# Weight parts with a buffer of their own, a last down projection in two portions, re-placed projections, and group 0's maxima by tiles

## The reference, cut to what matters

```python
x = x + _layernorm(_L0_attn_ref(_layernorm(x), ...))   # stage A: small 4-layer convolution net
x = x + _layernorm(_L0_ffn_ref(_layernorm(x), ...))    # stage B: silu(x W1) * (x W3), then W2, plus rank-2 parts
x = x + _layernorm(_L1_attn_ref(_layernorm(x), ...))   # stage C: causal attention, 32 heads of 32, 8 KV heads
x = x + _layernorm(_L1_ffn_ref(_layernorm(x), ...))    # stage D: x W_org plus 8 blended rank-64 updates

q = jnp.dot(x, Wq).reshape(b, t, H, HD).transpose(0, 2, 1, 3)
scores = jnp.where(causal, -jnp.inf, jnp.einsum('bhqd,bhkd->bhqk', q, k))
weights = softmax(scores * (1.0 / HD ** 0.5))
```

## Time and profile before

| | us |
|---|---|
| median of 3 runs | 2153.36 (2153.06 to 2156.35) |
| the profiled execution | 2154.8 |
| its span, first to last instruction | 2153.0 |
| PE busy | 2002.1 (93%) |
| DVE busy | 1423.2 (66%) |
| POOL busy | 1064.7 (49%) |
| ACT busy | 933.4 (43%) |
| mean granted clock of PE | 0.973 |

### The profile page before, as it was taken

How to read it: one execution, slowest core, us unless ns; L and a number is a source line. 1 busy time by engine, 2 the same in 40 slices (tenths; PEclk the granted TensorE clock), 3 DMA queues, 4 the chain that set the end, 5 groups by cost and what they waited for, 6 DMA issues and landing times. The chain is left out here.

```text
span 2153.0 us, 30681 instructions
## 1 busy us (share of the span) xinstructions
PE 2002.1 (93%) x10444; PEld 1451.0 (67%) x10444; DVE 1423.2 (66%) x3201; ACT 933.4 (43%) x1938; POOL 1064.7 (49%) x914
## 2 busy tenths in 40 slices
PE   5889886999999999989999899999998999999998
PEld 4644545778788878855666466665654687888887
DVE  7877667777777763177776477677776677654433
ACT  5645685333333323115554455555555433323211
POOL 1444586666666530008886488688884343220000
PEclk9999988999999999989999999999998999999999
DMA  6400376244444338532334643433253385543432
GB/s 188 173 9 1 121 232 230 94 151 167 162 167 167 123 129 305 156 95 57 79 81 111 188 117 80 113 98 97 64 165 117 95 271 183 180 168 132 142 123 97
DMA packets 153435, 292.12 MB, mean 136 GB/s; under 512 B 28750, under 2 KB 69582, under 8 KB 153152
## 3 DMA queue, kind: packets, MB, share of 16 engines
q1 hardware_dynamic: 124224, 241.93, 35.4%
q10 hardware_dynamic: 29056, 48.24, 6.8%
HBM read 163.48 MB, written 94.90 MB: 120 GB/s over the span
## 5 line engine op out<-in xcount | busy, mean ns | idle before, releaser
L2253 ACT ACTIVATE c_P<-PS 128x512 f32<-128x512 f32 (+3 forms) x768 | 349.1, 496 | 342.0 <-PE PS L2086 193.2
L2068 PE MATMUL PS<-c_K,c_Q 96*128 96x512 f32 (+3 forms) x768 | 276.8, 371 | 20.2 <-DVE cst L2385 8.8
L2086 PE MATMUL PS<-c_Q,c_K 97*128 97x512 f32 (+3 forms) x768 | 275.7, 373 | 17.1 <-ACT c_P L2253 9.8
L2498 POOL TENSOR_TENSOR c_S<-c_S,c_P 128x1024 f32<-128x1024 f32 (+3 forms) x94 | 242.0, 2575 | 20.3 <-DVE c_S L2334 12.9
L2086 PEld LDWEIGHTS PS<-c_Q,c_K 97*128 97x128 f32 x768 | 147.4, 193 | 140.0 <-ACT c_P L2253 96.3
L2381 DVE TENSOR_REDUCE cst<-PS 128x1 f32<-128x512 f32 x256 | 175.8, 687 | 77.0 <-PE PS L2068 76.7
L2068 PEld LDWEIGHTS PS<-c_K,c_Q 96*128 96x128 f32 x768 | 149.9, 195 | 77.0 <-DVE cst L2385 28.8
L214 POOL TENSOR_TENSOR maskw<-maskw,mhalf 128x1 f32<-128x1 f32 x64 | 37.7, 590 | 329.9 <-DVE maskw L172 317.6
L1432 DVE SCALAR_TENSOR_TENSOR b_pr<-b_g,b_a 128x460 f32<-128x460 f32 x192 | 180.8, 977 | 1.7
L2385 DVE CUSTOM_DVE_ANT_0 PS<-PS,maskw,cst 128x128 f32<-128x128 f32 (+3 forms) x256 | 142.8, 558 | 53.2 <-PE PS L2068 34.0
L2475 POOL TENSOR_SCALAR_AFFINE_SELECT c_P<-c_P 128x512 f32<-128x512 f32 x128 | 87.4, 683 | 159.8 <-ACT c_P L2253 159.8
(11 more groups left out here) (305 smaller groups left out, 4845.5 us busy)
## 6 DMA issues: line engine op xcount, KB each, us to landing
pre_d<-b_pre ACTq DMA_DIRECT2D x36, 512.0 KB, 2.8
c_w<-pre_d SPq DMA_DIRECT2D x34, 512.0 KB, 4.0
a_xin<-in_x SPq DMA_DIRECT2D x32, 512.0 KB, 4.3
d_x<-scr SPq DMA_DIRECT2D x32, 512.0 KB, 4.8
c_Q<-c_qh SPq DMA_DIRECT2D x240, 64.0 KB, 2.0
scr<-a_xin SPq DMA_DIRECT2D x16, 512.0 KB, 5.7
b_xn<-scr SPq DMA_DIRECT2D x16, 512.0 KB, 6.7
b_x<-scr SPq DMA_DIRECT2D x16, 512.0 KB, 5.8
```

The source lines that it names most:

```text
L2068: e.matmul(bank[:, 0:hi - lo], self.Q4[0:96, 4 * (o % 3) + g, 128 * t:128 * t + 128], self.K4[0:96, HEADS[o % 8], lo:hi], start=True, stop ...
L2086: e.matmul(self.k.bank(i % 3)[:, 0:hi - lo], self.K4[0:97, HEADS[o % 8], 128 * kt:128 * kt + 128], self.Q4[0:97, 4 * (o % 3) + g, lo:hi], ...
L2253: e.activation(self.P[:, R % 3, g, 0:hi - lo], self.k.bank(i % 3)[:, 0:hi - lo], ACT.Exp, scale=SCALE).then_inc(self.exp_s.s, 1)
L2498: e.tensor_tensor(S[:, gs, 512 - n:512], S[:, gs, 512 - n:512], P[:, gs, 0:n], ADD).then_inc(self.psum_s.s, 1)
```

## The change

1. Stage B: `raw` has a buffer of its own; a load waits only for the subtraction of the part before, the cast waits for the store. In ACT's list silu comes first, then the other work of the chunk, then cast, load and store of the parts; POOL's subtraction stands one chunk later. The two reductions of `dve_acc` share one `prod`, so the second waits for the first.
2. The end of stage B: `pe_gtr(15, 0)` stands ahead of the last chunk; the down projection runs in two portions, chunks 0 to 3 of both halves, then `pe_gtr(15, 1)`, then chunks 4 and 5.
3. Stage C's begin: group 0's maxima go by tiles (four heads of tile 0, then of tile 1, ...) from step 4 of projection 3 on, evenly over 27 steps (before: head by head, from step 10, over 22). The first 16 need only the first half of Q and K. SP places both halves of projection 0 ahead of the weight loads.
4. Slots: projections' second halves begin 2 slots later; K2, query 7, the reloads and most loads of the output weights move; `dve_job` stands one slot later; `late` and one `pool_mul` are set for group 5 too; stage D's tiles and splits move by 1 to 3 slots.

```diff
-            with nc.sbuf_tensor("b_raw", [128, 2, 512], F32) as raw:
-                self.raw = raw[:, 1, :]
+            self.raw = sb("raw", [128, 512])[:, :]
-            self.prod = [sb("pr0", [128, 460])]
-            self.prod.append(sb("pr1", [128, 460]))
+            self.prod = sb("pr1", [128, 460])
...
-    def pe_down(self, e, t, s):
+    def pe_down(self, e, t, s, pieces=range(6)):
         if s == 0:
-            e.wait_ge(*self.glo_s(2 * t + 2))
+            e.wait_ge(*self.glo_s(2 * t + (2 if 5 in pieces else 1)))
...
-        for i in range(2):
-            self.pe_gtr(e, 15, i)
+                if (t, c) == (15, 4):
+                    self.pe_gtr(e, 15, 0)
         for s in range(2):
-            self.pe_down(e, 15, s)
+            self.pe_down(e, 15, s, range(4))
+        self.pe_gtr(e, 15, 1)
+        for s in range(2):
+            self.pe_down(e, 15, s, (4, 5))
...
-        s = 6 * t + c - 9 - step
+        s = 6 * t + c - 10 - step
     def act_pre_load(self, e, p):
         if p > 0:
-            e.wait_ge(*self.pre_out(p))
+            e.wait_ge(*self.pre_lo(p))
     def act_pre_hi(self, e, p):
         e.wait_ge(*self.pre_in(p + 1))
+        if p > 0:
+            e.wait_ge(*self.pre_out(p))
...
-            if p > 0:
-                e.wait_ge(*self.u2_s(2 * p - 1 + r))
+            if p > 0 or r > 0:
+                e.wait_ge(*self.u2_s(2 * p + r))
...
-    return o, q_slots(48 * o - 112, 2, 48 * o - 94, 2), (48 * o - 95, 48 * o - 73)
+    return o, q_slots(48 * o - 112, 2, 48 * o - 92, 2), (48 * o - 95, 48 * o - 72)
-         ("K2", q_slots(208, 1, 219, 1), (217, 228)), (7, q_slots(231, 1, 243, 1), (242, 260)), ...
+         ("K2", q_slots(208, 1, 220, 1), (218, 233)), (7, q_slots(235, 1, 247, 1), (245, 262)), ...
-WO_IN = {644 + 6 * c: c for c in range(8)}
-TILES = {711 + 4 * n: (0, n) for n in range(8)} | {745 + 4 * n: (1, n) for n in range(5)}
+WO_IN = {643: 0} | {656 + 6 * c: c for c in range(1, 8)}
+TILES = {714 + 4 * n: (0, n) for n in range(8)} | {747 + 4 * n: (1, n) for n in range(5)}
-        late = 5 if S >= 720 or 432 <= S < 480 else 0
+        late = 5 if S >= 720 or 240 <= S < 288 or 432 <= S < 480 else 0
...
+    def max_of(self, o, a):
+        return (a % 4, MAXES[a // 4]) if o == 0 else (a // 12, MAXES[a % 12])
...
-            for o, a in ahead[max(0, 60 * (q - 10) // 22):max(0, 60 * (q - 9) // 22)]:
+            for o, a in ahead[max(0, 60 * (q - 4) // 27):max(0, 60 * (q - 3) // 27)]:
...
-                if S in self.evac_at:
-                    self.dve_job(e, *self.evac_at[S])
+                if S - 1 in self.evac_at:
+                    self.dve_job(e, *self.evac_at[S - 1])
-                if S == 704:
+                if S == 707:
                     for half in range(2):
                         self.then.dve_lo(e, 0, half)
...
-                if o > 0 and r in ((0, 7) if o in (9, 15) else (0, 4)):
+                if o > 0 and r in ((0, 7) if o in (5, 9, 15) else (0, 4)):
                     self.pool_mul(e, 2 * o - (2 if r == 0 else 1))
```

More of the change, by code:

```diff
@@ L1180, in pe_down @@
         o = self.k.bank(6 + s)
-        for c in range(6):
+        for c in pieces:
             a, b = self.gfh[0:115, c, :], self.gfl[0:115, c, :]
@@ L1340, in act @@
             for c in range(6):
-                last, now, p = (self.pre_at(t, c, step) for step in (2, 0, 1))
-                if last is not None:
-                    self.act_pre_store(e, last)
+                now, p, last = (self.pre_at(t, c, step) for step in range(3))
+                if (t, c) == (15, 5):
+                    self.act_ghi(e, 15, 0)
                 self.act_silu(e, t, c)
-                if p is not None:
-                    self.act_pre_hi(e, p)
                 if c in (0, 2):
@@ L1361, in act @@
                     T.act_x(e, t - 2)
+                if p is not None:
+                    self.act_pre_hi(e, p)
                 if now is not None:
                     self.act_pre_load(e, now)
+                if last is not None:
+                    self.act_pre_store(e, last)
                 if t == 1 and c == 5:
@@ L1369, in act @@
                     T.act_y(e, t - 1, y)
-        for i in range(2):
-            self.act_ghi(e, 15, i)
+        self.act_ghi(e, 15, 1)
         T.act_x(e, 14)
@@ L1429, in dve_acc @@
             a = 2 * C0[c] + n * r
-            if p > 0:
-                e.wait_ge(*self.u2_s(2 * p - 1 + r))
-            e.scalar_tensor_tensor(out=self.prod[r][:, 0:n], in0=g, scalar=0.5, in1=self.a2[:, a:a + n], op0=MUL, op1=MUL,
+            if p > 0 or r > 0:
+                e.wait_ge(*self.u2_s(2 * p + r))
+            e.scalar_tensor_tensor(out=self.prod[:, 0:n], in0=g, scalar=0.5, in1=self.a2[:, a:a + n], op0=MUL, op1=MUL,
                                    accum_out=self.u2[:, r, c:c + 1]).then_inc(self.u2_s.s, 1)
@@ L1491, in dve @@
                     self.dve_u2(e, t)
-        for i in range(2):
-            self.dve_glo(e, 15, i)
+        self.dve_glo(e, 15, 1)
         T.add(e, 14)
@@ L2058, in pe_turn, with max_of @@
         return self.turn_bank(o, a)
+    @staticmethod
+    def max_of(o, a):
+        return (a % 4, MAXES[a // 4]) if o == 0 else (a // 12, MAXES[a % 12])
     def pe_amax(self, e, o, a):
-        g, (t, lo, hi) = a // 12, MAXES[a % 12]
+        g, (t, lo, hi) = self.max_of(o, a)
         for part in range(2):
-            if a == 0:
+            if a == (16 * part if o == 0 else 0):
                 e.wait_ge(*self.placed[part](12 * o + 12))
-            if a == 0 and o in (0, 8, 12):
-                e.wait_ge(*self.k4[part]({0: 24, 8: 36, 12: 48}[o]))
+                if o in (0, 8, 12):
+                    e.wait_ge(*self.k4[part]({0: 24, 8: 36, 12: 48}[o]))
         bank = self.pe_turn(e, o, a)
@@ L2306, in act @@
                     self.then.act_hi(e, 0, (S - 699) // 2)
-                if S in (727, 743):
-                    self.then.act_hi(e, 1, int(S > 727))
+                if S in (728, 744):
+                    self.then.act_hi(e, 1, int(S > 728))
                 if S == 758:
                     self.then.act_y(e, 0)
-                if S == 760:
+                if S == 762:
                     self.then.act_hi(e, 2, 0)
```

27 lines of the change are left out of this document (15 added, 12 removed).

## The result

| | before | changed |
|---|---|---|
| median, us | 2154.64 (4 runs, 2153.06 to 2156.35) | 2129.70 (4 runs, 2128.92 to 2130.70) |
| span of the profiled execution | 2153.0 | 2127.7 |
| PE busy | 2002.1 | 1987.9 |
| DVE busy | 1423.2 | 1406.6 |

The ratio is 0.9884, 95% interval 0.9867 to 0.9901: 24.9 us less. Measured once more beside later experiments it was 0.9888 (0.9871 to 0.9904). The forecast was 2126.0, the range 2114 to 2140.

The account below looks back on a forecast made before the run. PE was taken as the bound, able to save only idle time and the half clock behind it. The terms summed to -27.7 us, 2127.1 from 2154.8 or 2125.7 from the median; the forecast was 2126.0, range 2114 to 2140.

Parts of the forecast that it names:

- Stage B: Stage B's weight parts: PE's waits for ACT's copy of the transposed input mostly go; -3.0 us, between -3.6 and +3.
- End of B: End of stage B: the split down projection delays DVE's list and PE idles 6.8 us; +5 us, between -1 and +7.
- Start of C: Start of stage C: maxima begin earlier, first score at about 948, SP ending last; -9.5 us, between -11 and -5.
- Group 5: Group 5, stage C: row of maxima issued ahead of K2, -7.7 us; POOL's sums ahead of its multiplication, -5.5 us.
- small waits for +2.5: New small waits from closer reloads and second halves two slots later: +2.5 us, a guess, between 0 and 5.
- Small waits in C: Stage C: splits on DVE stand behind the maxima a slot later, so PE waits less; -2 us, between -4 and +2.
- Group 14: Group 14, stage C: twelve slots without weight loads free its late row of maxima; -2 us, between -4.4 and 0.
- End of C: End of stage C: stage D's two splits go behind group 15's last maxima; -5.5 us, between -7.5 and -3.2.
- (a): Rival: start of C realised only by a third, projection 3's weights or SP's queue late; 2132.5 us, chance 0.12.
- (b): Rival: the end of stage B costs nothing, -1 instead of +5; 2120 us, chance 0.07.
- (d): Slower rival, stage B: ACT's casts wait for load and store, delaying PE's copy; +34 us, 2163, chance 0.05.
- (c): Rival: half of 22.7 us of removed stalls in stage C given back through POOL or DVE; 2138 us, chance 0.08.

Follow-up runs that it names:

- the second one with the list of before: The kernel before with only the first part of the change, stage B's buffers and order of ACT and POOL, against the kernel before: ratio 0.9978.
- the second trace of the same kernel: The changed kernel itself once more, unaltered, run beside the kernel with four edits: 2134.40 us, ratio to before 0.9888.

## Why the prediction was right, and where it was not

That the total came so near is in part luck: group 5 fell 7.5 us short of its terms, and smaller gains above forecast in stage B, at its end, at the start of C and at the end of C made up for 5.7 of that in this pair of traces. The largest of them, 2.9 us at the end together with group 14, is gone in four of the six other traces of the same list.

- **The bound.** PE's busy list is the same and the gain is waits and clock. Right.
- **Stage B.** Forecast -3.0; -3.9 in the first trace, and 421.0 as the mean of eleven traces with this part against the 424.2 of before, -3.2. The slower rival (casts waiting for load and store) was free of effect: ACT does wait for a store 12 times, 19.6 us, but behind the work that PE needs:

```profile
ACT b_g L1315 <- PE PS L1154: 58.5, 31, 4.9
...
ACT b_pre L1281 <- DMA pre_d<-b_pre: 19.6, 12, 2.0
```

  The step that failed is the price on DVE, which was in the bound only. I had up to 19 us more for the dependent reductions; they took less than before, 158.8 us busy and 5.0 idle against 179.3 and 1.7 for 190 of them:

```profile
L1437 DVE SCALAR_TENSOR_TENSOR b_pr<-b_g,b_a 128x460 f32<-128x460 f32 x190 | 158.8, 836 | 5.0
```

  From the start of the first to the end of the second, a pair has a median of 1.58 us in both kernels, so the wait between them costs nothing that shows. What fell is the time beside POOL. Before, 36 of the 95 pairs ran beside POOL's subtraction of a weight part and took 2.14 us on average, the others 1.74; with that subtraction a chunk later 12 pairs did and took 1.80, the others 1.70. The prediction had no term for that.
- **End of B.** Forecast +5, between -1 and +7; measured +3.9. The chain went as written: 6.71 us idle where I had 6.8. PE was about 3.5 us late at tile 2's transposes (forecast 4.1), and the half clock behind it cost 0.4 more than before (forecast 0.9). It did not cost more because PE's next wait, 1.64 us at tile 3, took most of it; the prediction had PE back to back there and nothing to absorb it. The row at 813.84 agrees with the sentence of the Trainium skill, "TensorE: Matmul & The Clock Gate", section "What's actually happening", on the throttled default state, which the prediction cites.
- **Start of C.** -9.5 forecast, -10.3 measured; first maximum and first score at the forecast times, and SP the last to end: it issued the row of maxima at 945.81, 2.4 us ahead of the first score. The other traces with this list took 162.3 to 165.5 us to r1, the second one with the list of before 170.4, so the gain lies between 4.9 and 10.8 us.
- **Group 5.** The step that failed is the split of terms into -7.7 and -5.5 with the clock's loss returned in both. The prediction asked what was late next only with "up to 1 us". It read that the chain on POOL was gone, and not that the same finish, five slots later, now has the reload beside it: a reciprocal one slot behind its load of 5 us, on the engine that makes the maxima. Of the 13.2 us 5.7 came in this pair of traces, and no more in any other.
- **K3.** The prediction had "second halves two slots later" among small waits for +2.5. It is +3.2 at one place, and its cause is a DMA that the placement is moved behind on SP. The prediction followed SP's order around K2 only, not around query 10.
- **Small waits in C.** -2 forecast, -2.5 in the stretches that no other term has. Between 1260 and 1600 PE's six waits for L2381 (2.0 us) are gone as forecast, but its waits for POOL's sums rose from 0.6 to 3.9 us.
- **Group 14.** -2 forecast, nothing found: 1.36 us idle instead of 1.37. Loads at 662 and 668 still lay beside the row, which is issued at slot 664; with them away the row was in time, and ACT and POOL were not.
- **End of C.** -5.5 forecast; group 14 and the end together gave 10.4 in the first trace but 2.0 in the second trace of the same kernel (138.6 against 140.7). What differs is the wait for the row (1.36 and 2.43 us) and the clock behind it, below. r15 parts the two terms. From r15 to the last score seven traces took 45 to 47 us against 52 before, and the wait of 3.24 us ahead of r15 is gone too: the end gave some 8 to 10 us, more than its 5.5. From r13 to r15 without that wait it was 85.8 us before and 85.2 to 91.7 after: group 14 gave at most 0.6 and mostly lost, where it was to give 2. The two errors have opposite signs, and that their sum is near the forecast of -7.5 is luck. The wait and the 6.8 us at half clock behind it make 3.24 + 3.4 = 6.6 us of the end's gain; where the rest comes from no run shows. The prediction's reading of the earlier trace rows as 2.37 us for each subtraction was wrong as well: they took 4.13 and 0.68.
- **The rivals.** (a), (b) and (d) did not come. (c), removed stalls given back, came in group 5, through DVE, for 7.5 us, and in most traces in group 14, through ACT. Its 22.7 us are those of groups 5, 14, the end and the small waits; without the last they are 20.7.

## What to carry to other kernels

When a step is moved by a slot, look on every queue at what it passes: one slot on SP put twelve DMAs behind a transfer that waits for another engine, and cost more than 2 us. When a stall goes, search for the next wait on the engine that works in order behind it, and count a small transfer at what it takes beside the bulk transfers of its new time, not at its usual time. And if two waits lie in one chain, moving one alone may show nothing: the total of the stretch tells more than the wait that went.
